# One pipelined hybrid-attention kernel: the loop over slots replaced by all slots written out

## The reference

```python
x = x + attn_a(layernorm(x))   # 16 heads of 64: q = relu(x Wq)+eps, k = relu(x Wk)+eps, causal linear attention, Wo, bias
x = x + ffn(layernorm(x))      # rows quantised to int8, times a quantised 512x512 matrix, scaled back
x = x + attn_b(layernorm(x))   # 16 heads of 32: rotary q and k, rank-16 maps, a gated state that decays,
                               # M = M * decay + (g k) v^T ; y = q M, then out_w, a residual and a layer norm
x = x + ffn(layernorm(x))
```

## Time and profile before

| | us |
|---|---|
| three runs, median | 3124.61 (3123.05 to 3124.82) |
| the profiled execution, its span | 3127.1 |
| of it PE busy | 3004.2 |
| DVE busy | 2367.4 |
| POOL busy | 1044.8 |
| ACT busy | 744.8 |

### The profile page before, as it was taken

One profiled execution on the slowest core, in us unless ns is written; L12 is line 12 of the kernel. 1 busy time (PEld: TensorE's weight loads), 2 busy tenths in 40 slices (PEclk: granted clock), 3 DMA queues, 4 the chain that ended last, 5 costly groups with the idle time before them and its releaser, 6 DMA issues.

```text
span 3127.1 us, 126889 instructions
## 1 busy us (share of the span) xinstructions
PE 3004.2 (96%) x54866; PEld 2270.9 (73%) x54932; DVE 2367.4 (76%) x5409; ACT 744.8 (24%) x1357; POOL 1044.8 (33%) x1398
## 2 busy tenths in 40 slices
PE   3699999999999999999999999999999999999995
PEld 2577777777777777777777777777777777777663
DVE  6867777777777777777777777777777777777775
ACT  2222222222222222222222122222222222222211
POOL 2023333333333333333333333333333333333333
PEclk9799999999999999999999999999999999999997
DMA  5212222222232222322222222222222222222210
GB/s 173 67 39 49 44 45 51 42 50 46 42 51 44 46 48 46 50 42 47 49 42 48 48 46 45 48 45 45 51 43 49 47 42 51 44 46 48 46 40 24
DMA packets 384396, 153.91 MB, mean 49 GB/s; under 512 B 352800, under 2 KB 361632, under 8 KB 383904
## 3 DMA queue, kind: packets, MB, share of 16 engines
q1 hardware_dynamic: 383904, 146.02, 24.8%
HBM read 45.29 MB, written 16.78 MB: 20 GB/s over the span
## 4 chain that ended last, share of the span: by engine, by line
PE 93%; DVE 4%; issue 1%; DMA 1%; ACT 0%; POOL 0%; SPq 0%; DVEq 0%; POOLq 0%; ACTq 0%
PE bank L752 22%; PE bank L753 21%; PE bank L754 21%; PE bank L1038 8%; PE bank L917 3%; PE bank L832 3%; PE bank L870 3%; PE bank L990 2%; PE bank L710 2%; PE bank L847 2%; PE bank L889 2%; PE bank L1013 2%; PE bank L1000 1%; DVE absmax L1177 1%; PE bank L1026 1%
## 5 line engine op out<-in xcount | busy, mean ns | idle before, releaser
L672 POOL TENSOR_TENSOR work<-work 128x512 f32<-128x512 f32 x128 | 185.6, 1450 | 659.2 <-DVE work L1433 659.2
L752 PE MATMUL bank<-xaT,wq_hi 128*128 128x128 f16 x2048 | 359.9, 220 | 6.3 <-DVE wk_lo L1202 4.0
L753 PE MATMUL bank<-xaT,wq_hi 128*128 128x128 f16 x2048 | 359.9, 220 | 0.0
L754 PE MATMUL bank<-xaT,wq_lo 128*128 128x128 f16 x2048 | 359.9, 220 | 0.0
L752 PE MATMUL bank<-xaT,wk_hi 128*128 128x128 f16 x2048 | 358.8, 220 | 0.0
L753 PE MATMUL bank<-xaT,wk_hi 128*128 128x128 f16 x2048 | 358.6, 220 | 0.0
L754 PE MATMUL bank<-xaT,wk_lo 128*128 128x128 f16 x2048 | 358.5, 220 | 0.0
L752 PE MATMUL bank<-xbT,wb 128*128 128x128 f16 x2048 | 348.3, 220 | 0.0
L753 PE MATMUL bank<-xbT,wb 128*128 128x128 f16 x2048 | 347.6, 219 | 0.6 <-issue 0.6
L754 PE MATMUL bank<-xbT,wb 128*128 128x128 f16 x2048 | 347.5, 219 | 0.0
L1322 DVE TENSOR_SCALAR work<-bank,eps_q 128x256 f32<-128x256 f32 x256 | 123.0, 481 | 178.7 <-PE bank L754 178.7
(11 more groups left out here) (210 smaller groups left out, 8243.0 us busy)
## 6 DMA issues: line engine op xcount, KB each, us to landing
xin<-in_L_attn_a_x SPq DMA_DIRECT2D x64, 256.0 KB, 2.6
out<-xf SPq DMA_DIRECT2D x64, 256.0 KB, 2.1
table<-in_tables SPq DMA_DIRECT2D x64, 192.5 KB, 2.6
work<-in_L_attn_a_Wq SPq DMA_DIRECT2D x1, 2048.0 KB, 7.9
work<-in_L_attn_a_Wk SPq DMA_DIRECT2D x1, 2048.0 KB, 12.9
wb<-in_L_attn_a_Wv SPq DMA_DIRECT2D x1, 2048.0 KB, 17.6
work<-in_L_attn_a_Wo SPq DMA_DIRECT2D x1, 2048.0 KB, 8.4
work<-work SPq DMA_TRANSPOSE x128, 3.9
```

The source lines that it names most:

```text
L672: pool.tensor_tensor(to[:, :, :, :], to[:, :, :, :], cross[:, :, ::-1, :], ALU.add)\
L752: nc.tensor.matmul(o, a[0], b[0], start=first, stop=False)
L753: nc.tensor.matmul(o, a[0], b[1], start=False, stop=False)
L754: return nc.tensor.matmul(o, a[1], b[0], start=False, stop=last)
```

## The change

```diff
@@ -476,13 +476,7 @@
                             if piece in late:
                                 late[piece]()
 
-            for s in range(FIRST_LOOP_SLOT):
-                walk(Slot(eng, s))
-            with nc.Fori(FIRST_LOOP_SLOT // 2, CHUNKS // 2, engines=[eng.engine], hint_back_edge=True) as it:
-                registers = {(per, const): eng.snap(it * per + const) for per, const in COUNTS[name_of]}
-                for n in range(2):
-                    walk(Slot(eng, n, it, registers))
-            for s in range(CHUNKS, CHUNKS + MAX_LAG):
+            for s in range(CHUNKS + MAX_LAG):
                 walk(Slot(eng, s))
 
         WEIGHTS = {"q": (SQ, Wq, wa["q"]), "k": (SK, Wk, wa["k"]), "v": (SV, Wv, wa["v"]), "o": (SO, Wo, wo),
```

## The result

| | median us | runs |
|---|---|---|
| before | 3124.45 | 3123.05 to 3124.82, 4 runs |
| changed | 3153.89 | 3149.61 to 3156.82, 4 runs |
| ratio | 1.0092 | 95% interval 1.0078 to 1.0106 |

The change costs 29.4 us. I forecast slower, but 11.6 us of it, and the time lies 7.9 us over the upper end of my range.

The account below looks back on a forecast made before the run. TensorE's own stream was taken to bound the kernel. From 3127.1 us, 19.6 for packet-edge gaps was added and 8.2 for loop, exit and stretch 60 removed; less 2.5 from span to median gave 3136.0 us, range 3122 to 3146.

Parts of the forecast that it names:

- The bound: Whole kernel: TensorE's own instruction stream sets the time, 46.42 us a stretch if always fed; other engines set nothing.
- the cause: Dense part of a stretch: TensorE waits where a 16 KB packet of 128 matmul-load pairs ends; a stretch counts 870.
- the walk of 26 places a stretch: Written-out stretches: 7 times 128 less 870 moves the packet edge 26 places each stretch, giving a pattern of five.
- the clean families: Stretches with the packet edge at places 142 to 162 or 168 to 188, 21 of them: cost 0.
- the worth of the loop: Marks 7 to 59: registers, entry and 25 taken branches cost 3.6 us together, which go with the loop.
- Rival 1: No stalls, faster: the early gaps belong to the beginning, only the 8.2 us go; 3116.4 us, chance 0.07.
- Rival 2: Partly hidden: only places 220 to 240 stall, or stalls are shorter; 3118 to 3127 us, chance 0.12.
- Rival 3: Slower by the clock: gaps nearer 1.75 us at places 194 to 214 lower TensorE's clock; 3151 us, chance 0.09.
- The term for places 194 to 214: Stretches 8, 13, ..., 58 (11): stall begins near place 198, reaches 0.9 us by 202; 7 us, bounds 1.5 and 9.3.
- The term for places 220 to 240: Stretches 9, 14, ..., 59 (11): mean gap 0.84 us from three measured; 9.3 us, bounds 7.9 and 11.3.
- gaps elsewhere: Sign of being wrong: gaps other than at L870, L889 or the first L752 to L754 behind them.
- the exit: Stretch 59, behind the last branch: 50.07 us, 3.65 us too long from an idle gap and lower clock; taken out whole.

Follow-up runs that it names:

- free156: The changed kernel plus 52 already satisfied wait instructions a stretch behind 512-column matmul groups, holding the packet edge at place 156; 3121.76 us, 0.9991 of the kernel before.

## Why the prediction was right in kind and wrong in size

**What was right.** The bound (TensorE's stream alone), the cause (edges of 128 pairs, a stretch of 870), the walk of 26 places a stretch and so which stretches would have gaps, the clean families, and the worth of the loop: 3.6 us. From mark 7 to mark 59 free156 takes 2413.84 us where before took 2417.40. Rival 1, no stalls, needed padding to come true. Rival 2, one family alone, is out too: three families had gaps. Rival 3, the clock, did not come: it is granted in full from mark 7 to mark 60, with gaps of up to 1.5 us. TensorE written out alone has a gap of 1.76 us and keeps its clock too, so the length of a gap alone does not decide it. The Trainium skill ("Runtime: NRT & Kernel Launch", Instruction fetch mechanics) has a taken branch as the thing that stalls the fetch, and the crossing of a block in straight code as mostly hidden. The runs here show straight code 29 us slower than the loop and, once its edges are held, 3.4 us faster.

**Where the 17.9 us went.** The measured median lies 17.9 us over my 3136.0. The gaps cost 30.8 us and not 19.6: 11.2 us. Stretch 60, from which I took 1.0 us off, takes 38.91 us where it took 37.41: 2.5 us. It waits for other engines as well, and TensorE written out alone, with the same edges, takes 36.1 us for it, so its length cannot be read off one gap. What comes before mark 7 and behind mark 61 is 4.4 us shorter in all, which I had not forecast. The remaining 8.6 us lie in the step from a profiled span to a median: I took 2.5 us off, and the median lies 6.1 us over the span.

**The term for places 194 to 214, 7 us forecast, 13.2 measured.** This is the step that failed. I had the point where it begins (198) and the wrong price: I called the range between places 192 and 218 unmeasured, gave the gap 0.85 us, in the middle of the prices at 218 to 244, and let it grow towards that from nothing. The packets say otherwise. Here is the DMA's share in 40 slices of 0.1 us, from 826 us for stretch 13 (place 196, mark at 817.54) and from 1063 us for stretch 18 (place 198, mark at 1052.95):

```profile
DMA  9400000000000002000006000000000000000000
...
DMA  0000000000000000000005000000000000000000
```

The packets start at 828.1 and 1065.1, that is 10.6 and 12.2 us behind their marks. From place 198 on nearly all start 12.2 to 12.9 us behind the mark, wherever the edge is, and work goes on 2.2 to 2.9 us after the start. So the gap is about 12.4 + 2.4 less the time at which TensorE is at the edge: 13.2 us at place 198, 13.8 at 218, 14.7 at 244. By that the gap is longest at the first place and shrinks from there. Measured, a stretch has 1.3 to 1.7 us too much at places 198 to 210, 1.16 at 212, 1.05 at 214 and 0.72 at 218. Stretch 18 on TensorE's timeline:

```profile
1065.80 0.53 PE L864 MATMUL bank<-va,work 64*64 64x65 f32 x22
1067.45 0.45 PE L864 MATMUL bank<-va,work 64*64 64x65 f32 x13 [1.12 <-issue]
```

I had both numbers in hand, the packet's start behind the mark (12.1 for place 218) and 2.35 us to its use, and TensorE's time at each place. Taken together they give 1.2 us at place 198 and 0.8 at 214, some 9.6 us for the nine, already over my upper bound of 9.3.

The trace of before even had a gap in this family. By the count of matmuls, the 1.75 us in L870 of stretch 59 stand at place 199 and the 1.03 us in stretch 60 at place 225: 26 places on, the step that I had worked out. The packet began 12.4 us behind the mark, and work went on 2.0 us later than in a stretch without a gap. I booked this gap as a cost of the loop's exit and took it out, when it was the price of the family that I called unmeasured. The kernel with only the other engines written out has the same gap, and it costs 1.5 us there; nine of these make 13.5.

**The term for places 220 to 240, 9.3 forecast, 12.4 measured.** Priced from three gaps. In this execution the packets for places 230 to 240 began 12.8 us and more behind the mark, in earlier stretches (places 220 to 228) 12.4, and the excess of stretches 34 to 59 is 1.15 to 1.5 us each. Three samples were too few for an upper bound of 1.03.

**A dense part that I left out: 3.7 us.** A stretch has a second one, places 713 to 856 (L1020, L1007, L826). I looked for edges in the first alone; "gaps elsewhere" was one of my signs of being wrong, and here it holds. When the edge is at place 222 or 224 of a stretch, another is at 855 or 856. On TensorE's timeline in stretch 14:

```profile
913.17 0.27 PE L826 MATMUL bank<-work 64*64 64x64 f32 x1 [1.34 <-issue]
```

A few places later the f32 matmuls of L1032, 0.43 us each, give the packet time, and the gap is gone.

**What I took off for the exit, and the 2.5 us.** A program's time is 1.8 us over its span in the profiled execution of the changed kernel (3149.61 and 3147.8). If that holds for before too, its profiled execution took 3128.9 and not 3124.6: it was a long one, and the 3.65 us of stretch 59 are probably part of why, since the kernel with only the other engines written out shows 1.5 us there. If so, I took some 2 us of this excess off twice, once as part of the 8.2 us and once with the 2.5 us.

**The spread.** The changed kernel's four runs reach over 7.2 us, the four of before over 1.8; but the 21 runs of before beside free156 reach over 7.3. The profiled execution of the change was the fastest. Span against span the change costs 20.7 us, median against median 29.4. Where the remaining 4 us of the slower executions went no trace here shows. Two things are seen to differ between traces. The gaps do: TensorE alone written out has more excess in single stretches (28 with 2.0 us, 19 with 3.2), though over stretches 7 to 58 it takes only 1.9 us more than the change. And the time up to mark 0 does: it lies between 210.3 and 215.3 us in the traces of this case.

**What stays open.** Why the packet for an edge behind place 198 begins no earlier than 12.2 us behind the mark, 1.2 us after the dense part's start, no run shows; the increments are not it.

## What to carry to other kernels

A long stream of small matmuls is fed by packets of instructions, and where a packet's edge falls among them decides whether TensorE waits: measure the time from a packet's start to its use and compare it with the time that TensorE needs for the matmuls of one packet. Before writing out a loop, count the instructions of a pass; if the count is no multiple of the packet, edges walk through every part of the body, and if it is, they stay where they are put. When an edit only moves code, and a kernel with the same work differs by per cents, count instructions up to the gaps before looking for a cause in the engines.

## What was not expected of the hardware

- 156 instructions that run once, in front of a loop, made the kernel 155 us slower, by moving the loop's packet edges by 78 places (156 of the 160 us of the profiled execution lie in the loop).
- A semaphore increment or an already satisfied wait on TensorE has a row of 51 ns, but the next one starts only 0.151 us (increment) or 0.106 us (wait) later. 13 increments turned 0.86 us between pairs of f32 matmuls into 2.0; 28 waits among the same matmuls cost 0.3 us a stretch, and 24 between 512-column matmuls nothing.
- Eight such increments ahead of small matmuls cost 0.06 us a stretch.
- A packet of instructions takes 0.9 to 1.9 us on q8, and TensorE goes on 2.2 to 2.9 us after it starts.
